# Another order on VectorE, ScalarE and GpSimd in the second stage of an attention, LSTM and FP4 feed-forward kernel

## The reference, cut to what matters

```
def lstm(x, h, Wx, Wh, b):            # x: 64 x 64 x 256, h = cond, c = 0
    for t in range(64):
        a = x[:, t] @ Wx + b + h @ Wh
        i, f, o = sigmoid(a[:, 0:256]), sigmoid(a[:, 256:512]), sigmoid(a[:, 512:768])
        c = f * c + i * tanh(a[:, 768:1024])
        h = o * tanh(c);  hs[:, t] = h

def fp4_quant_dequant(x):             # blocks of 16 along the last dim
    scale = max(max|x| of the block / 6, 1e-12)
    return nearest of {0, .5, 1, 1.5, 2, 3, 4, 6} to |x / scale|, with its sign, * scale

gate, y = q(hs) @ q(w_gate).T, q(hs) @ q(w_up).T        # 256 -> 704, q = fp4_quant_dequant
out = x + q(silu(gate) * y) @ q(w_down).T               # 704 -> 256
```

## Time and profile before

| | us |
|---|---|
| median of 3 runs (lowest, highest) | 1059.73 (1059.33, 1062.59) |
| the profiled execution's own time | 1062.53 |
| its span, first to last instruction | 1060.5 |
| busy in the span: PE, DVE, ACT, POOL | 895.4, 920.3, 506.7, 344.2 |

### The profile page before, as it was taken

The page is one execution under the profiler, slowest core; times in us unless marked ns, Lnnn a source line. Parts: engine busy times, 40 slices in busy tenths (PEclk is TensorE's granted clock), DMA queues, the critical chain, the costliest instruction groups (busy, mean ns, idle before and its releaser), DMA issues.

```text
span 1060.5 us, 27568 instructions
## 1 busy us (share of the span) xinstructions
PE 895.4 (84%) x9862; PEld 599.7 (57%) x9862; DVE 920.3 (87%) x2157; ACT 506.7 (48%) x1177; POOL 344.2 (32%) x436
## 2 busy tenths in 40 slices
PE   3477887988988888888987899999999999999974
PEld 1254654766666666666654555565565556555542
DVE  5489889899999999999984689888888988888883
ACT  2256446466666666667653334434333343433321
POOL 0135456355555555555542011110111111111111
PEclk9589679799999999999998999999999999999987
DMA  4501000010111001110110000000000000000000
GB/s 104 190 13 29 19 19 29 23 33 18 32 32 32 28 21 32 32 32 21 30 31 16 1 11 21 21 21 20 20 16 15 21 20 21 20 20 19 15 19 25
DMA packets 37143, 30.37 MB, mean 29 GB/s; under 512 B 12081, under 2 KB 35953, under 8 KB 37076
## 3 DMA queue, kind: packets, MB, share of 16 engines
q1 hardware_dynamic: 37076, 29.42, 9.9%
HBM read 20.87 MB, written 8.54 MB: 28 GB/s over the span
## 4 chain that ended last, share of the span: by engine, by line
PE 22%; DVE 15%; issue 8%; ACT 4%; POOL 1%; DVEq 0%; POOLq 0%; ACTq 0%
PE bank L987 6%; PE bank L711 5%; PE bank L886 4%; PE bank L875 4%; DVE fc L1461 4%; DVE hqT L1523 2%; DVE h_value L171 2%; ACT hqT L1182 2%; DVE ig L1463 2%; DVE x_value L171 1%; DVE cell L1465 1%; ACT h L1157 1%; POOL ffn_room L663 1%; PE bank L979 1%; PE bank L866 1%
## 5 line engine op out<-in xcount | busy, mean ns | idle before, releaser
L663 POOL TENSOR_TENSOR ffn_room<-h_value,h_scale 128x704 f32<-128x704 f32 x32 | 45.7, 1428 | 382.0 <-DVE h_value L171 382.0
L711 PE MATMUL bank<-gu,xqT 128*128 128x512 f16 (+1 forms) x576 | 130.1, 366 | 0.0
L886 PE MATMUL bank<-wh,h 128*64 128x512 f16 x768 | 95.1, 383 | 1.9 <-ACT h L1157 1.9
L875 PE MATMUL bank<-wx,x1T 128*64 128x512 f16 x768 | 93.8, 379 | 0.9 <-DVE x1T L440 0.9
L611 POOL TENSOR_TENSOR p<-prob,p 128x520 f16<-128x520 f32 x64 | 78.7, 1230 | 43.2 <-ACT p L1065 43.2
L1147 ACT ACTIVATE sig<-bank 128x256 f32<-128x256 f32 x64 | 24.6, 384 | 139.5 <-PE bank L886 138.9
L987 PE MATMUL bank<-dn,hqT 128*128 128x256 f16 x576 | 71.5, 280 | 22.5 <-DVE hqT L1523 22.5
L875 PEld LDWEIGHTS bank<-wx,x1T 128*64 128x64 f16 x768 | 78.5, 201 | 11.6 <-DVE x1T L440 1.2
L711 PEld LDWEIGHTS bank<-gu,xqT 128*128 128x128 f16 x576 | 54.4, 99 | 52.8 <-issue 11.3
L1461 DVE TENSOR_TENSOR fc<-sig,cell 128x128 f32<-128x128 f32 x64 | 52.4, 818 | 34.4 <-ACT sig L1147 34.4
L776 PE MATMUL bank<-ident,p 128*65 128x128 f16 x1024 | 78.8, 228 | 1.5 <-POOL p L611 0.8
(11 more groups left out here) (201 smaller groups left out, 2220.9 us busy)
## 6 DMA issues: line engine op xcount, KB each, us to landing
x_in<-in_x SPq DMA_DIRECT2D x32, 128.0 KB, 2.2
x_res<-in_x SPq DMA_DIRECT2D x32, 128.0 KB, 2.1
x_rows<-x_rows_sb SPq DMA_DIRECT2D x32, 128.0 KB, 1.9
ffn_room<-x_rows SPq DMA_DIRECT2D x64, 64.0 KB, 2.2
out<-ffn_room SPq DMA_DIRECT2D x64, 64.0 KB, 2.0
mask_in<-in_mask_Bx1x1xS_ff SPq DMA_DIRECT2D x64, 16.0 KB, 2.4
x1T<-in_L_cond_Wx SPq DMA_DIRECT2D x1, 1024.0 KB, 6.5
x1T<-in_L_cond_Wh SPq DMA_DIRECT2D x1, 1024.0 KB, 8.5
```

The source lines that it names most:

```text
L663: pool.tensor_tensor(blocks(hq, FF), blocks(fp4_h.value, FF), spread(fp4_h.scale, FF), ALU.mult).then_inc(s["hq_ready"], 1)
L711: last = pe.matmul(dst, lhs(a, c), rhs(b, c), start=first and c == 0 and a == b, stop=c == C - 1 and (a, b) == parts3[-1], skip_group_chec ...
L875: last = pe.matmul(bank[e][B * h:B * h + B, :], x1T16[m][:, c, :, at], half_cols(wx16, a, c, h), start=False, stop=True, skip_group_check= ...
L886: last = pe.matmul(bank[e][B * h:B * h + B, :], h16[:, m, c, :], half_cols(wh16, a, c, h), start=False, stop=True, skip_group_check=True)
```

## The change

Nothing that is computed changes, nor do PE's, SP's and GpSimd's programs. DVE's pipeline gets a fifth tile in flight: the last addition of a tile, now in `store_rows`, is done one step later (t5), directly behind the first `lstm_cell`. Step 4 of `quant_h` moves from the start of a step to the end of the one before. Steps 5 and 6 of `quant_h` now run together ahead of `quant_x` steps 1 to 4 and of `lstm_lo`; `silu` comes ahead of step 5 of `quant_x`, and its step 6 behind the second `lstm_cell`. `xqT`'s low part comes behind `quant_h` steps 1 to 3. On ACT the magnitude of h goes ahead of the tanh of the first half step, and the gate's sigmoid ahead of the magnitude of x.

```diff
 ACT
             if t1:
                 lstm_gates(t1, 0)
-                lstm_tanh(t1, 0)
             if t4:
                 act.wait_ge(s["quant_h"], t4.count(Fp4.SCALED, Fp4.STEPS))
                 fp4_h.magnitude(act, FF).then_inc(s["magnet_h"], 1)
             if t1:
+                lstm_tanh(t1, 0)
                 lstm_hi(t1, 0)
-            if t2:
-                act.wait_ge(s["quant_x"], t2.count(Fp4.SCALED, Fp4.STEPS))
-                fp4_x.magnitude(act, D).then_inc(s["magnet_x"], 1)
             if t3:
...
+            if t2:
+                act.wait_ge(s["quant_x"], t2.count(Fp4.SCALED, Fp4.STEPS))
+                fp4_x.magnitude(act, D).then_inc(s["magnet_x"], 1)
 DVE
+        def store_rows(t):
+            q = t.parity
+            dve.wait_ge(s["down_ps"], t.count())
+            dve.wait_ge(x1_loaded[q], mask_count(t))
+            after(dve, out_stored[q], out_count(t))
+            dve.scalar_tensor_tensor(out=out_rows[:, q, :], in0=pair67[:, FFC * P:FFC * P + D], scalar=1.0 / W_D,
+                                     in1=x1_res[:, q, :], op0=ALU.mult, op1=ALU.add).then_inc(s["out_ready"], 1)
+
         def step(tiles):
-            t1, t2, t3, t4 = tiles
+            t1, t2, t3, t4, t5 = tiles
             if t1:
                 lstm_cell(t1, 0)
-            if t4:
-                quant_h(t4, [4])
+            if t5:
+                store_rows(t5)
             if t1:
                 lstm_h(t1, 0)
+            if t4:
+                quant_h(t4, [5, 6])
             if t2:
...
-                quant_x(t2, range(1, 4))
+                quant_x(t2, range(1, 5))
             if t1:
                 lstm_lo(t1, 0)
-            if t2:
-                quant_x(t2, [4])
-            if t4:
-                quant_h(t4, [5])
-            if t2:
-                quant_x(t2, [5])
-            if t4:
-                quant_h(t4, [6])
-            if t2:
-                quant_x(t2, [6])
-            if t1:
-                lstm_cell(t1, 1)
             if t3:
... (silu)
+            if t2:
+                quant_x(t2, [5])
+            if t1:
+                lstm_cell(t1, 1)
+            if t2:
+                quant_x(t2, [6])
             if t1:
                 lstm_h(t1, 1)
... (hqT low part, hid)
+            if t1:
+                lstm_lo(t1, 1)
+            if t3:
+                dve.wait_ge(s["hid_ready"], t3.count())
+                after(dve, s["hq_ready"], t3.count(back=1))
+                quant_h(t3, range(1, 4))
             if t2:
... (xqT low part)
-            if t1:
-                lstm_lo(t1, 1)
-            if t3:
-                dve.wait_ge(s["hid_ready"], t3.count())
-                after(dve, s["hq_ready"], t3.count(back=1))
-                quant_h(t3, range(1, 4))
... (the old place of what store_rows does)
-        pipeline(dve, 4, step, first=6)
+            if t3:
+                quant_h(t3, [4])
+
+        pipeline(dve, 5, step, first=6)
```

More of the change, by code:

```diff
@@ L1529, in step @@
                                          op0=ALU.mult, op1=ALU.mult).then_inc(s["hid_ready"], 1)
[L1530 to L1533, removed]
             if t1:
@@ L1539, in step @@
                 quant_h(t3, range(1, 4))
[L1540 to L1546, removed]
-        pipeline(dve, 4, step, first=6)
+            if t2:
+                dve.wait_ge(s["xqT_hi"], t2.count())
+                dve.tensor_tensor(by_chunk(xqT16[:, 1, :]), by_half(bank[2][:, D:2 * D]), by_chunk(xqT16[:, 0, :]),
+                                  ALU.subtract).then_inc(s["xqT_lo"], 1)
+            if t3:
+                quant_h(t3, [4])
+        pipeline(dve, 5, step, first=6)
 def kernel(**inputs):
```

## The result

| | before | changed |
|---|---|---|
| median, us (range, 4 runs each) | 1059.53 (1058.06 to 1062.59) | 1043.08 (1040.71 to 1044.04) |
| ratio, 95% interval | | 0.9832 [0.9813, 0.9852] |
| span of the profiled execution | 1060.5 | 1040.8 |

The forecast was 1046 in a range of 1038 to 1056. The changed kernel is 16.5 us (1.7%) faster, and the interval of the ratio stays clear of 1.

The account below looks back on a forecast made before the run. Bound: a chain of waits through ACT, DVE and PE. Period 13.48 + 0.34 = 13.82 against 14.25; 29 periods give 12.5 us, the end 1.5: gain 14 from the median 1059.73, forecast 1046, range 1038 to 1056.

Parts of the forecast that it names:

- What bounds the kernel: Second stage: a chain of waits through ACT, DVE and PE sets the period of 14.25 us a tile.
- The floor of 13.48: Shortest period PE's order allows: transposes at 8.67, chain of 2.74, down products of 2.07; 0.77 below today's 14.25.
- (a): GpSimd's products moved beside instructions without two SBUF inputs: fc and ig fall to 0.29, and 0.77 a period goes.
- the slower rival: The product of h holds x step 3 or 4 ahead of lstm_lo: PE waits 1.20, about 1071 us; chance 0.10.
- The parts, 0.38 each: Split of the 0.77 above the floor: 0.38 at PE's transposes, 0.39 in the chain to the down products.
- (b): First half step: magnitude of h, some 0.8, ahead of tanh, which starts at 3.03 instead of about 2.83; 0.2 hidden.
- (c): Second state products on PE: a new wait of 0.34 for lstm_lo, which moves everything behind it.
- (d): Second half step: fc unstalled, chain the bare 2.74, DVE idle some 1.2 ahead of hqT, 0.5 to spare before fc.
- The sum: Whole kernel: 12.5 us from the periods plus 1.5 at the end, a gain of 14 us.
- The 29 periods: Steps 3 to 31, all four tiles in flight: each 0.43 shorter, 12.5 us together.
- At the start: First steps, set by the LSTM's own chain: no change, at worst a loss of 0.5.
- At the end: Last three steps, DVE and GpSimd in one chain: gain between 0 and 2.7, taken as 1.5.

Follow-up runs that it names:

- e3: The changed kernel with lstm_lo of the first half step moved ahead of quant_x steps 1 to 4 on DVE: 1037.2 us, ratio 0.9783.
- e1: The kernel before, with GpSimd's product of h waiting until the second ig of the step is done: 1074.11 us, ratio 1.0124.
- e2: The changed kernel with quant_x step 6 directly behind step 5, ahead of the second cell: 1040.01 us, ratio 0.9848.
- e9: The changed kernel with GpSimd's product of h held until the state products of the second half step: 1048.47 us, ratio 0.9906.
- e8: The changed kernel with two extra GpSimd products a tile, released with the gates of the second half step: 1147.35 us, ratio 1.0854.
- e6: The changed kernel with one extra GpSimd product a tile, released with the gates of the second half step: 1062.12 us, ratio 1.0049.

## Why the prediction was right, and where it was off

*What bounds the kernel: right.* A period is PE's order, plus what PE waits for at three places. The floor of 13.48 was met by e3 within 0.06 (13.49 and 13.58). The stalls of `fc` and `ig`, 1.6 a period, cost 0.3 to 0.4 there, through the late tanh (e1); where the tanh still comes in time, a stall of 0.3 (e2) or of 1.1 (`fc` in e9) makes the chain no longer.

*(a), the products: right.* No x step is longer beside GpSimd, so the slower rival is out on the trace: step 3, the one form without a row, took 0.26 as always. PE's wait at L979 is gone and the chain shorter. The parts, 0.38 each by my working, are seen in e9 only roughly: the early product is worth 0.32, the rest of the change together 0.19, the gain of the chain less the new wait for `lstm_lo`.

*(b), the first half step: mis-sized.* I had the tanh start 0.80 behind the magnitude. It starts 0.68 behind it. This is the main reason that the period is 13.74 and not 13.82: `lstm_lo` starts 817.89 - 811.37 = 6.52 behind the state products, not 6.63.

*(c), PE's new wait: right in place, too large in size.* Forecast 0.34, measured 0.16 to 0.25 (1.65 and 1.74 against 1.49). e3 gave it back: 13.745 - 13.535 = 0.21.

*(d), the second half: right.* DVE idles 1.28 ahead of `hqT` (forecast 1.2) and 0.46 to 0.54 ahead of the first `fc` (0.5). The chain measured 823.13 - 820.29 = 2.84, in the period before 2.76, against 2.74.

*The sum: 14 forecast, 16.5 measured by the medians, 17.9 by the parts of the two profiles.* The medians lie nearer to the forecast than the two profiles do only because executions of one kernel differ, here by 3 to 5 us. The 29 periods brought 14.8 instead of 12.5. The two ends were sized worse, and in opposite ways. At the start I had allowed a loss of 0.5 at most and there is one of 1.1: in step 2 nothing of h is to be done yet by the old order, while the new one puts h step 4 ahead of the next `fc`, and that step takes 11.60 instead of 10.75. At the end I had 1.5, in bounds of 0 to 2.7, and it is 4.2, outside the bounds and a quarter of the whole gain. The largest part is in the first step without the LSTM, 13.4 us before and 10.7 now, where GpSimd's product comes earlier (timeline of PE in the changed kernel, then the transposes in the kernel before):

```profile
1003.57 2.76 PE L711 MATMUL bank<-gu,xqT 128*128 128x512 f16 x12 [0.68 <-DVE xqT L1542]
...
1008.57 0.88 PE L979 MATMUL bank<-ident,ffn_room 128*128 128x128 f32 x6 [2.23 <-POOL ffn_room L663]
```

```profile
1025.90 1.54 PE L979 MATMUL bank<-ident,ffn_room 128*128 128x128 f32 x6 [4.02 <-POOL ffn_room L663]
```

Before, PE waited 4.02 at that place, not 2.23, and the same six transposes then took 1.54 and the down products 3.12, where they take 0.88 and 2.71 now. I had counted DVE's instructions there and not PE's clock: the granted clock over that step was 0.75 and is 0.84. How much of the 4.2 is clock and how much order was not tried apart.

## What to carry to other kernels

In these runs a stalled instruction cost what it delayed on the way to the next place where the bounding engine waits, and not its own length. So write the period down as that engine's order with its waits, then put the partner engine's product where its result is early and its neighbours use at most one SBUF input. When a reordering removes one wait, look for the next in the same queue; here moving `lstm_lo` and the transposes, found by the same sum, brought another 2% (0.9607 against 0.9832).

## What the runs showed of the hardware that was not expected

- The clock of TensorE fell inside a period in which PE was busy for 86 of 100 us. In e8, after a wait of 1.9 us and one of 0.4, the down products ran at a granted clock of 0.57 and took 3.56 instead of 2.14. In the step before the first slow one, with waits of 1.88 and 0.45, they still took 2.14. In e1, with 1.12 and 0.66, and in e6, with 0.56 and 0.38, the clock stayed at 1.00. What decides between these cases was not tried.
- A GpSimd product is held by a VectorE instruction as well, by less than the rest of that instruction: in e6 the extra product took 1.84 instead of 1.68, where a two-input instruction of 0.42 had begun 0.13 before it. In e9 the product of h took 1.47 instead of 1.39, where one had begun 0.19 before it.
- On ScalarE the tanh started 0.12 before the recorded end of the activation of 704 columns ahead of it, since it had nothing to wait for (813.57 + 0.80 against 814.25).
